# One output sum kept in PSUM, one vector step split over three engines, and a norm stage moved beside attention

## What is computed

```python
x = x + gated_delta(layernorm(x))   # 16 key heads, 32 value heads, DK = DV = 128, conv of 4 taps
x = x + mlp(layernorm(x))           # 256 -> 512 -> 512 -> 256, relu
x = x + attention(layernorm(x))     # 4 heads of 64, no mask
x = x + moe(layernorm(x))           # rms norm, 32 experts, top 4, shared expert
# gated_delta, per head and token:
state = state * exp(g)
delta = (v - k @ state) * beta
state = state + outer(k, delta)
out   = q @ state                   # then * silu(z), rms norm, @ w_out
```

## Time and profile before

| | before |
|---|---|
| time of three runs, us | 1553.78, 1554.52, 1560.2 |
| the profiled execution, us | 1565.12, of which the span is 1563.3 |
| PE busy | 1346.6 us, 86% |
| VectorE busy | 1024.9 us, 66% |
| ScalarE busy | 778.6 us, 50% |
| GpSimd busy | 751.7 us, 48% |
| mean granted clock of TensorE | 0.927 |

### The profile page before, as it was taken

The page is one execution under the profiler, slowest core; times in us unless marked ns, Lnnn a source line. Parts: engine busy times, 40 slices in busy tenths (PEclk is TensorE's granted clock), DMA queues, the critical chain, the costliest instruction groups (busy, mean ns, idle before and its releaser), DMA issues. The chain is left out here.

```text
span 1563.3 us, 24959 instructions
## 1 busy us (share of the span) xinstructions
PE 1346.6 (86%) x8680; PEld 908.1 (58%) x8680; DVE 1024.9 (66%) x1958; ACT 778.6 (50%) x1915; POOL 751.7 (48%) x1226
## 2 busy tenths in 40 slices
PE   6687988989898898988989898899797799697994
PEld 3365655666565566656666665666545356453673
DVE  6865877787786877878787786966522266541354
ACT  3454756566565655646566564765432265210121
POOL 1774674756658476664756648572100000025263
PEclk9878989889998999989989998999999899889997
DMA  3513335343543535345343543545300870112387
GB/s 92 141 32 101 85 119 128 88 114 85 161 103 101 122 88 141 92 127 133 88 117 93 150 109 98 119 121 161 106 1 1 324 191 1 61 53 100 71 187 187
DMA packets 233181, 171.72 MB, mean 110 GB/s; under 512 B 163746, under 2 KB 202998, under 8 KB 230240
## 3 DMA queue, kind: packets, MB, share of 16 engines
q1 hardware_dynamic: 226912, 161.59, 37.8%
q0 software_dynamic: 6144, 8.53, 3.0%
HBM read 104.64 MB, written 65.83 MB: 109 GB/s over the span
## 5 line engine op out<-in xcount | busy, mean ns | idle before, releaser
L803 PE MATMUL psum_banks<-main_hT,gdn_w_in 128*128 128x512 f32 x512 | 247.1, 608 | 16.5 <-DVE heads_y L1286 10.4
L1286 DVE SCALAR_TENSOR_TENSOR heads_y<-psum_banks,gdn_conv_w,heads_y 128x1021 f32<-128x1021 f32 (+2 forms) x192 | 245.1, 1277 | 9.8 <-ACT heads_y L1099 4.8
L1579 POOL TENSOR_TENSOR heads_XT<-heads_XT,heads_tmp 128x126 f32<-128x126 f32 (+22 forms) x496 | 201.2, 406 | 38.9
L1576 POOL TENSOR_TENSOR heads_tmp<-heads_XT,heads_A 128x126 f32<-128x126 f32 (+22 forms) x496 | 191.9, 387 | 43.6 <-PE psum_banks L968 4.0
L803 PEld LDWEIGHTS psum_banks<-main_hT,gdn_w_in 128*128 128x128 f32 x512 | 93.8, 193 | 97.3 <-issue 77.1
L917 PE MATMUL psum_banks<-heads_w_z,main_hT 128*128 128x256 f32 x512 | 146.6, 438 | 0.0
L832 PE MATMUL psum_banks<-heads_S,heads_kT 128*128 128x256 f32 x224 | 77.3, 429 | 67.9 <-DVE heads_S L1307 66.1
L1561 POOL TENSOR_TENSOR heads_v_s<-heads_v_s,heads_k_root 128x2048 f32<-128x2048 f32 x16 | 58.2, 3638 | 158.4 <-DMA heads_v_s<-values_by_tokens 158.4
L1307 DVE SCALAR_TENSOR_TENSOR heads_S<-heads_S,heads_coef,psum_banks 128x128 f32<-128x128 f32 x192 | 57.2, 339 | 98.6 <-PE psum_banks L857 98.2
L917 PEld LDWEIGHTS psum_banks<-heads_w_z,main_hT 128*128 128x128 f32 x512 | 108.7, 223 | 21.8 <-issue 6.2
L2120 POOL DMA_INDIRECT expert_rows<-moe_rows,route_dest x32 | 31.4, 980 | 185.8 <-DVE route_dest L2099 176.3
(11 more groups left out here) (280 smaller groups left out, 3048.2 us busy)
## 6 DMA issues: line engine op xcount, KB each, us to landing
values_by_tokens<-heads_v_s SPq DMA_DIRECT2D x64, 256.0 KB, 4.1
heads_v_s<-values_by_tokens SPq DMA_DIRECT2D x16, 1024.0 KB, 5.7
outputs_by_features<-heads_ogT SPq DMA_DIRECT2D x120, 128.0 KB, 3.8
heads_ogT<-outputs_by_features SPq DMA_DIRECT2D x30, 512.0 KB, 4.1
main_w_gu<-in_w_gu SPq DMA_DIRECT2D x4, 2816.0 KB, 20.8
gdn_w_in<-in_w_in SPq DMA_DIRECT2D x16, 512.0 KB, 4.5
heads_A<-kk_blocks SPq DMA_DIRECT2D x64, 128.0 KB, 4.9
keys_by_tokens<-heads_k_tok SPq DMA_DIRECT2D x64, 128.0 KB, 3.2
```

The source lines that it names most:

```text
L803: ins = pe.matmul(out[:, half * 512:(half + 1) * 512], w_in[:, kd_, j * P:(j + 1) * P], hT[:, kd_, half * 512:(half + 1) * 512], start=kd_ ...
L1286: dve.scalar_tensor_tensor(y[j][:, shift:T], src[:, 0:T - shift], conv_w[:, head, j, t:t + 1], y[j][:, shift:T], ALU.mult, ALU.add).then_i ...
L1576: pool.tensor_tensor(tmp[:, 0:n, 0:m], bc_last(XT[:, 0:n, j], m), bc_mid(A0[:, j, j + 1:BLK], n), ALU.mult).then_inc(solve_step.sem, 1)
L1579: pool.tensor_tensor(XT[:, 0:n, j + 1:BLK], XT[:, 0:n, j + 1:BLK], tmp[:, 0:n, 0:m], ALU.add).then_inc(solve_step.sem, 1)
```

## The change

It has three parts.

First, in the scan the sum of the two output terms stays in `bank_b`: DVE adds `O1` in PSUM and multiplies from there by the gate. For c = 0 the copy is gone. `b_free` is given after the multiplication, not after the sum; `og_ready` is gone and ACT waits on `b_free`.

Second, for every head but the first, the diagonal is taken by ACT (new piece `diagonal`), the factor `cb` is made by POOL, and DVE keeps the reciprocal and the transpose. `scales` moves from row 12 to 13, `norms` from 13 to 14, `attn1` on DVE from 12 to 16, and other pieces by a row or so. `gates` on SP's queue moves behind `outputs_out0`.

Third, the semaphores of `heads` (97) are cleared by POOL inside attention's first block, and attention's are not cleared. The fourth norm is done tile pair by tile pair in attention's last block, on DVE, ACT and PE, with POOL adding `ln` to `x`. The prefetch is issued at the start of `route_and_share`, first `w_r`, then `sw_gu`.

```diff
 PE_PLAN
-0: z0/0 p0/-1
-1: p1/-1
+0: z0/2
+1: p0/-1 p1/-1
...
-9: attn0/1
-10: p4/-1 attn1/2
+10: p4/-1 attn0/1
 11: y6a/3 y6b/0
-12: p5/-1
+12: attn1/2 p5/-1
...
-16: y7_0/0 p6/-1
-17: p7/-1
-18: y7_1/3 u7_0/0
+16: p6/-1 y7_0/0 u7_0/0
+17: y7_1/3
+18: p7/-1
 ACT_PLAN
-0: q_silu z0 q_square
-1: base0
-3: v0_silu
-4: v1_silu keys z1 z2
-7: exp0 gamma kk0 base1 exp1 exp2
-8: kk1
-9: exp3
...
-13: base2 u6a norms
+0: z0 q_silu base0 q_square v0_silu
+3: v1_silu z1
+4: keys z2
+7: exp0 gamma kk0 base1 kk1 exp1 exp2
+10: exp3
...
+13: base2 diagonal
+14: norms u6a
 DVE_PLAN
-7: factors
-8: decay3 tap10
-9: tap11 tap12 turn
+9: tap10 tap11 tap12 decay3
+10: factors turn
 11: attn0 ot0
-12: attn1 scales
+13: scales
 14: tap20 tap21
 15: tap22 ot1
+16: attn1
-SP_PLAN = """kt_out inverse_out gates kt_in inverse_in values_out products_out values_in products_in
-outputs_out0 w_z outputs_in0 outputs_out1 outputs_in1 w_in w_o""".split()
+SP_PLAN = """kt_out inverse_out kt_in inverse_in values_out products_out values_in products_in outputs_out0
+gates outputs_in0 w_z outputs_out1 w_in outputs_in1 w_o""".split()
@@ heads, scalar
+            def block_diagonal(h):
+                act.wait_ge(blk_loaded.sem, blk_loaded.end(h) * 16)
+                act.wait_ge(cb_step.sem, cb_step.base(h))
+                act.activation(nd[:], flat(A0[:])[:, 0:BLK * BLK:BLK + 1], ACT.Copy, bias=EPS, scale=-1.0).then_inc(cb_step.sem, 1)
@@ heads, vector, scan_quantum part 2
-                    if c == 0:
-                        dve.tensor_copy(mine, bank_b[:, 0:2]).then_inc(b_free.sem, 1)
-                    else:
-                        dve.tensor_tensor(mine, bank_b[:, 0:2], O1[:], ALU.add).then_inc(b_free.sem, 1)
-                    dve.wait_ge(b_free.sem, b_free.done(h, f"o{c}"))
-                    dve.tensor_tensor(mine, mine, gate, ALU.mult).then_inc(og_ready.sem, 1)
+                    if c:
+                        dve.tensor_tensor(bank_b[:, 0:2], bank_b[:, 0:2], O1[:], ALU.add).then_inc(o_summed.sem, 1)
+                        dve.wait_ge(o_summed.sem, o_summed.done(h, f"o{c}"))
+                    dve.tensor_tensor(mine, bank_b[:, 0:2], gate, ALU.mult).then_inc(b_free.sem, 1)
@@ heads, gpsimd, eliminate
-                pool.wait_ge(cb_step.sem, cb_step.done(h, "cb"))
+                if h:
+                    pool.wait_ge(cb_step.sem, cb_step.done(h, "rnd"))
+                    pool.tensor_tensor(cb[:], rnd[:], beta_rows[:, h], ALU.mult).then_inc(cb_ready.sem, 1)
+                pool.wait_ge(cb_ready.sem, cb_ready.done(h, "it"))
@@ attention, first block, gpsimd
                 pool.memset(zeros[:], 0.0).then_inc(s_zero, 1)
+                for s in used_sems:
+                    pool.sem_clear(s)
@@ attention, last block, tensor, after outputs(3)
+                for half in range(2):
+                    ...
+                    for t in range(4 * half, 4 * half + 4):
+                        pe.wait_ge(s_xn, t + 1)
+                        for kd in range(KD):
+                            ins = pe.transpose(turn_bank[half][kd][:, t % 4], rows[:, t, kd * P:(kd + 1) * P], ident[:])
+                    ins.then_inc(s_turned, 1)
@@ attention, last block, scalar
                 rows_out(BLOCKS - 1)
+                for u in range(NT // 2):
+                    roots(u)
+                    normalise(u)
+                    if u == 2:
+                        act.wait_ge(s_turned, 1)
+                        act.activation(hT[:, 0, 0:512], turn_bank[0][0].rearrange("p a b -> p (a b)"), ACT.Copy).then_inc(s_ht, 1)
@@ attention, last block, vector
+                for u in range(3):
+                    statistics(u)
+                    shifts(u)
+                    if u:
+                        scaled(u - 1)
                 feats_out(BLOCKS - 1)
-                for u in range(NT // 2):
-                    dve.wait_ge(s_o, u + 1)
-                    xs = x[:, 2 * u:2 * u + 2].rearrange("p a b -> p (a b)")
-                    dve.tensor_tensor(xs, xs, out_bank[u], ALU.add).then_inc(s_add, 1)
-                dve.wait_ge(s_add, NT // 2)
-        a.clear_sems()
+                scaled(2)
+                statistics(3)
+                shifts(3)
+                scaled(3)
@@ route_and_share, sync
+            prefetch(sp)
```

More of the change, by code:

```diff
@@ L305 @@
 7: exp0 exp1 exp2 exp3 base3
-11: norms
+11: diagonal norms
 13: y6a y6b
@@ L375, in belongs @@
         return h in FINISH and h <= HK
-    if name.startswith(("kk", "p", "solve", "base", "tap", "keys", "norms", "scales")):
+    if name.startswith(("kk", "p", "solve", "base", "tap", "keys", "norms", "diagonal", "scales")):
         return h in AHEAD
@@ L1816, in _ @@
                 outputs(3)
+                for half in range(2):
+                    if half == 0:
+                        for i in range(2):
+                            pe.wait_ge(s_pt[i], 2 * R)
+                    else:
+                        pe.wait_ge(s_add, 2)
+                    for t in range(4 * half, 4 * half + 4):
[3 more added lines that the diff above has]
+                    ins.then_inc(s_turned, 1)
             @block.scalar
@@ new lines, in scaled @@
+                def scaled(u):
+                    mine = slice(2 * u, 2 * u + 2)
+                    dve.wait_ge(s_root2, u + 1)
+                    dve.reciprocal(rstd2[:, mine], root2[:, mine]).then_inc(s_rstd2, 1)
+                    dve.wait_ge(s_rstd2, u + 1)
+                    if u == 0:
+                        dve.wait_ge(s_norm, 16)
+                    for t in (2 * u, 2 * u + 1):
+                        dve.wait_ge(s_ln, t + 1)
+                        dve.scalar_tensor_tensor(rows[:, t, 0:D], ln[:, t], rstd2[:, t:t + 1], w_norm, ALU.mult, ALU.mult).then_inc(s_xn, 1)
```

192 lines of the change are left out of this document (120 added, 72 removed).

## The result

The changed kernel took 1478.76 us in the median of 4 runs (1475.01 to 1479.38), the kernel before 1556.33 us in 4 runs beside it (1553.78 to 1560.2). The ratio is 0.9495, with a 95% interval from 0.9467 to 0.9522: faster by 77.6 us, where 1490 us was forecast and 1450 to 1535 given as the range. The profiled execution took 1475.01 us, with a span of 1473.2 us against 1563.3.

A forecast was written before the change was run, and what follows sets the result against it. PE was taken as the bound, losing time to one wait and the half clock behind it. From the median of 1554.5, 58 + 53 - 34 - 18 + 5 - 3 = 61 gave 1493; forecast 1490 us, range 1450 to 1535.

The forecast's parts named there:

- The wait at L832 goes, 58 us: PE's wait for the state at chunk 5's keys' product disappears, 14 x 4.1 = 58 us gained.
- The half clock behind it, 53, of which 18 come back: PE's half clock after that wait goes, gaining 53 us; new idle time brings it back in one head in three, costing 18.
- The pair of waits: PE waits of 1.24 and 1.49 us, 1.1 us of work between, taken as enough to bring the clock down.
- New idle time, 34 us: New PE waits in the reordered head rows raise idle time from 2.2 to 4.5 us a head, costing 34 us.
- The walk: One head traced through the new rows with durations from the timeline; it gave 60.1 us a head.
- Diagonal: cover of 1 us: Key blocks land at about 606, ACT reaches the diagonal at 606.9: no new wait, about 1 us to spare.
- The rivals in which the wait only moves, or grows: ACT or VectorE waits instead, 1550 to 1560 us, chance 0.06; or key blocks land over 7 us later, slower, chance 0.06.
- Output sum in PSUM, -3: VectorE's savings in the scan not counted as gain; the later product costs 8 x 0.4 = 3 us in the last scan.
- Semaphores, 6.8 us: Before attention, 97 clears move to GpSimd inside attention, hidden by the products there: 6.8 us.
- Fourth norm, 0 within 2.5 us: In attention's tail, the earlier norm and the later w_r load cancel up to the router's block, within 2.5 us.
- Profiled against median: Profiled execution lay 10.6 us above the median of 1554.5; the summed microseconds were subtracted from the median.
- the marks named: Expected profile: longest in-head wait for chunk 3's Dl, 2 to 2.5 us; head 60 to 63 us; PEclk 0.95 to 1.

The follow-up runs named there:

- the sum alone: Kernel before with only the output sum written back into PSUM and multiplied by the gate from there: 1534.09 us, ratio 0.9841.
- the rows alone: Kernel before with only VectorE's scales moved from row 12 to 13 and ScalarE's norms from 13 to 14: 1519.06 us, ratio 0.9744.
- The bolder spreading: Changed kernel with last features early, ScalarE's kk1, exp1, exp2 in row 9, third tap and p4 in row 11: 1490.57 us, ratio 0.9582.
- the kernel without the split: Changed kernel with the diagonal and the product of scales and beta back on VectorE in every head: 1479.43 us, ratio 0.949.

## Why the prediction was right, and where it was off

- *The wait at L832 goes, 58 us.* Right. It was 4.08 us a head from 202 to 1005 us, and none is left in the middle heads. The cause that was named, the scales ahead of the state update, was one of two. Moved alone, the scales left a stand of 3.6 us at the gated output, and the gain was 40 us instead of the 58 + 53.
- *The half clock behind it, 53, of which 18 come back.* The net of 35 was near. PE's busy time a head fell from 60.4 to 58.2 us, 14 x 2.3 = 32 us. Both terms were too large: full clock is 57.45 us, so there were 3.0 us to gain and not 3.8. The clock fell in 5 of 12 middle heads, more often than the one in three, but that cost 0.7 us a head on average and not 1.3. The pair of waits that the estimate went by the earlier trace rows is no clean sign: from 1005.4 to 1006.7 us, in front of it, PE had only 96 matmuls of 32x32 to do. One fall shows in these windows of about a microsecond (the columns of the earlier trace rows):

```profile
431.43:432.00 0.57, 0.57 (x4) 0.57 (x4) 0.57 (x1) 0.57 (x4) 0.00 (x0) 0.75 0.38 61
432.00:433.00 1.00, 1.00 (x4) 0.89 (x4) 0.92 (x2) 0.63 (x5) 0.00 (x0) 0.50 0.78 115
...
434.00:435.00 1.00, 1.00 (x3) 0.48 (x2) 0.96 (x4) 0.00 (x0) 0.12 (x1) 0.50 1.03 426
435.00:436.00 1.00, 1.00 (x4) 0.49 (x4) 0.97 (x2) 0.00 (x0) 1.00 (x2) 0.94 0.97 401
```

  3.4 us at half clock cost 1.7 us, against 7 to 10 us at half clock behind the old wait of 4 us.
- *New idle time, 34 us.* This is the term that was off. Outside the long wait, PE's idle time went from 2.3 to 3.2 us a head, 14 x 0.9 = 12 us and not 34. The walk had 4.5 us in five waits where 3.2 came, also in five. The largest was nearly right, 2.25 us for `Dl` of chunk 3 against 2.06. `Dl` of chunk 1 is late by 0.31 us and not 0.85. Around chunks 5 and 6 the walk had three waits of 0.4 to 0.5 us; there are two, both at chunk 5, of 0.27 and 0.30, and the fifth is one of 0.27 at the `X` of chunk 1, which was there before. The wait of p4 for the taps, 0.74 us before, is gone, because PE comes to p4 later; the walk had none there either. So what failed is the length of the waits: 1.3 us a head too much, 18 us, and with the 2.2 taken for 2.3 and 2 us for the first head 22 us. Against them lie 3 us in the clock's net; the rest nearly cancels. The sum had 61 us where the profiled executions, without the stand, differ by 79.6, and its median of 1493 is 14 above the measured one.
- *Diagonal: cover of 1 us.* It was more than that. ScalarE's diagonal (0.25 us) has no idle time before it in any middle head, and the key blocks land 2.2 to 4.1 us ahead of it. The rivals in which the wait only moves, or grows, needed that one.
- *Output sum in PSUM, -3.* Wrong in sign. The rows for it were read rightly, down to the operations of GpSimd that end with VectorE's. What failed was the step "it isn't the bound, so this counts only where it stood before `X`, in the wait that is booked above": there was a second wait behind the booked one, that of L845, and alone the edit gave 24 us. In the whole change it is worth 4 us at most. The 3 us of loss booked for the last scan didn't come: from the first gate product of the last head to its last `o` it is 38.0 us before and with the sum alone, and 38.3 in the changed kernel. The scan before it is 2.2 us longer than it was (51.5 and 49.3 us). The sum doesn't do that: in the old orders this scan takes 49.6 us with the sum alone, 48.9 with the rows alone and 49.3 with both. PE idles less in it than before and is busy for 3.0 us more, at a granted clock of 0.93 where it was 1.00. Why the clock falls there stays open.
- The PSUM to PSUM form took 426 ns, at the lower bound of 416 to 630. The product from PSUM takes 422 ns and its old form takes 424 at its shortest. The Trainium skill (VectorE: DVE Perf Modes, the section on the TRN2 errata) gives a PSUM source a larger fixed cost; these rows don't show it.
- *Semaphores, 6.8 us.* Right: from the last copy of `hT` at 1132.21 to the first product are 2.4 us, and 9.4 before. The product:

```profile
1134.64 1.19 PE L1686 MATMUL psum_banks<-main_hT,main_lend 128*128 128x512 f32 x1 [3.44 <-PEq L55]
```

- *Fourth norm, 0 within 2.5 us.* Its steps came as told: root at 1268.9, 134.3 us behind attention's first product, and the last features 9.6 us behind that. The router's product comes 157.95 us behind attention's first, and 155.68 before: +2.3, and the shared expert's +4.1, more than the 2.5 us allowed.
- *Profiled against median.* The profiled time of before lay 10.6 us above the median, and the stand in the shared expert's stage is 10.5 us. To subtract it was right; a look at that stage would have shown where it lay.

Of the marks named: the longest wait is for `Dl` of chunk 3 (2.06), a head takes 60.7 to 62.4 us, the clock is 0.97 and 1, and the gated output never takes over 0.43 us. All came.

## What to carry to other kernels

When an operation takes twice its usual time beside another engine's, find its partner before moving anything. Moving the victim away only exposes the next operation in line, and several cures of one stand don't add up: 40, 40 and 24 us alone were some 75 together. A walk through new rows finds the places of the waits better than their lengths: here four short ones came out 0.5 us a head or less too long, and over 14 heads that was most of the error. And an engine that is busy 80% of the time can still be the chain for a few microseconds of each round; here, taking an independent product from in front of its wait cost more than the wait that it removed elsewhere.

## What the hardware showed

*VectorE and GpSimd.* The 128x256 product of two SBUF operands takes 0.42 us alone and up to 3.86 us beside GpSimd's 3.64 us scaling; the 32-column diagonal takes 0.18 alone and up to 2.55. All those shown end within 0.3 us of GpSimd's operation. With one operand in PSUM the same product is never over 0.43, and the convolution taps (one operand in PSUM) are 1.23 to 1.29 us always. The Trainium skill has it (SBUF — State Buffer, the section "Who interferes with whom"): a VectorE instruction with two SBUF inputs contends with a GpSimd instruction that reads SBUF, whoever comes first keeps the shared port to its end, and one with at most one SBUF input outside the two-port modes doesn't contend. These runs agree, the 0.18 and 2.55 of the diagonal, which has one SBUF input, being the two-port case by the page. It would have priced the output sum.

*The clock.* In middle heads with one wait of 2.06 us it fell in 5 of 12; with one of 1.0 and, 2 us later, one of 0.77 in 4 of 12; with one of 1.0 and one of 0.3 in none. The bolder spreading had none over 1.42 but idle time of 4.4 us a head, and it fell in 6 of 12; the kernel without the split had one of 2.06 again, and it fell in 3 of 12. Heads with the same waits differ, so the waits alone don't tell which head is hit, nor does the longest wait. Of these kernels the one with the least idle time a head, 2.75 us, kept its clock; why the heads of the others differ among themselves stays open.
